# A four-direction selective scan on one core: transposes in place of products, and the 24 units of a chunk and their side jobs in another order

## The chip, the cores and the metric

The kernel runs on one core of a Trainium2 chip. The core has five engines that run their own instruction streams and meet only at semaphores: TensorE (PE; its weight loads are shown apart as PEld), VectorE (DVE), ScalarE (ACT), GpSimd (POOL) and SyncE (SP), which only issues DMAs here. SBUF is the working memory, PSUM takes TensorE's results. The metric is the device time of one execution in microseconds (us), and of several executions the median.

## The reference, cut to what matters

Layer 0 normalises x, projects it, convolves it, and then runs a selective scan over the 4096 pixels of each of 8 images, in four directions k (rows, columns, and both backwards). For each of 192 channels d and 16 states n:

```
delta = softplus(dt_proj(x_dbl) + bias)          # per channel and pixel
A     = -exp(A_logs)
h     = exp(delta * A) * h + (delta * u) * B     # over the pixels, one state per (d, n)
y     = sum over n of h * C
out   = y + u * D                                # the four directions are added at the end
```

B and C (16 values per pixel each) and the six inputs of `dt_proj` come from a projection of u with its own weights in each direction. A gated projection back to 96 channels and a second layer follow; the change touches neither.

## The kernel before

The program has three phases, one after the other: before the scan, the scan (`scan_phase`) and after it. Only the scan phase is changed. Its work is cut into 128 **chunks** (8 images, 4 directions, 4 pieces of TC = 1024 pixels). A chunk is two **steps** n, the even and the odd one, of 96 channels each. A step is 12 **units** x = 0 to 11, so a chunk has 24, which the prediction counts 0 to 23 (unit 12 is unit 0 of the odd step). A unit is a tile of 128 partitions by 1024 pixels: 32 channels (j = x mod 3) by 4 states (g, from the table `ORDER`).

What a unit costs on the engines depends on its kind (`KIND`):

- **Direct** (14 of 24): TensorE spreads B over the partitions into one of two PSUM tiles P (`fill`, 2 matmuls, L597), VectorE multiplies it with dt*u (`multiply`, L717), ScalarE makes the decay E (`exp`, L823), and VectorE runs the recurrence (`scan`, L739).
- **Diagonal** (6): TensorE makes the product itself, with 32 small matmuls of transposed dt*u (dluT) by diagonal copies of B (diag) (L639); VectorE only scans. These wait for `lt_copied` and `diag_made`.
- **Pooled** (4): GpSimd multiplies dt*u by B (L905) into one of two tiles dbu, ScalarE puts the decay into P; VectorE only scans, TensorE fills nothing.

After the scan GpSimd multiplies each H by C (`weigh`, L913), ScalarE saves the last column (`carry`, L829), and TensorE sums three units at a time into y (`sum_y`, L661; two halves in two iterations, in the third none; at the start of a step with one more matmul, L652 or L655).

The buffers that tie the engines together: P has 2 tiles, so the fill of unit un waits for the scan of un - 2 (`scan_done`); E has 3, H has 4 (a scan waits for `weigh` of un - 4), HC has 7, dbu has 2.

Once or twice a chunk come the **side jobs**. They go through one PSUM tile, `stage`, so each waits for ScalarE's copy of the one before (`held`): `project` (L581: B, C and dt inputs of the next chunk, a read of u that is strided for the odd directions), `delta` (L591, then softplus on ScalarE with a table load before and after, L773), `turn_b` (L610), `rep` 0 to 4 (L597: B or C spread over all partitions; the list `REPS` says which) and `turn_dlu` (L620: dt*u transposed, once a step). After `project` ScalarE copies twice (L763, L764) and VectorE takes the rounding rest (`split`, L711). ScalarE makes 32 diagonal copies a chunk (`diagonal`, L807), and GpSimd makes dt*u (`delta` in `pool`, L896), which goes out to DRAM and comes back spread over partitions (SP's queue).

Every engine's order is written out by hand: a loop over the units in which `if x == ...` says where each side job stands. TensorE's iteration un is: fill of unit un + 1, a half of `sum_y`, side jobs. Nothing overtakes anything on its engine.

Of the kernel before, what the change touches and what calls it, by code (L numbers as in the profile page):

```python
# [16 lines left out]
C = 96  # L17
# [291 lines left out]
def scan_phase(nc, ctx, T, S):  # L309
# [9 lines left out]
    DIAG_EVEN, DIAG_ODD = {0: 3, 1: 4, 2: 4, 3: 4}, {6: 3, 7: 3, 8: 3, 9: 3, 10: 2, 11: 3}  # L319
# [151 lines left out]
    for n in range(NSTEP):  # L471
        c = n // 2 + 1
        if n % 2 == 0:
            order += [("rep", c - 1, i) for i in range(3, 5) if n] + [("lt", n + 1)]
            order += [("x", c)] if c < NCHUNK else []
        elif c < NCHUNK:
            order += [("dt", n + 1), ("bt", c), ("rep", c, 0), ("lt", n + 1), ("dt", n + 2), ("rep", c, 1), ("rep", c, 2)]
# [6 lines left out]
    def sync(e):  # L484
# [62 lines left out]
        for n in range(NSTEP):  # L547
            if n % 2 == 0:
                if n:
                    in_dlr(n + 1)  # L550
                    out_dlu(n + 1)
                if ends_image(n + 1) and n + 2 < NSTEP:
                    load_u(n // 32 + 1)
                if n:
                    in_dur(n + 1)
                    store_y(n - 1)
                load_y(n + 1)
            else:
                if n + 1 < NSTEP:
                    out_dl(n + 1)  # L560
                    in_dlr(n + 1)
                store_y(n - 1)
                if n + 1 < NSTEP:
                    out_dlu(n + 1)
                    in_dur(n + 1)
# [6 lines left out]
    def tensor(e):  # L572
# [41 lines left out]
        def turn_dlu(m, sub):  # L614
# [63 lines left out]
        for un in range(NUNIT + 12):  # L678
# [7 lines left out]
            if n % 2 == 0:  # L686
                if x < 2 and n:
                    rep(c - 1, x + 3)
# [5 lines left out]
            elif c < NCHUNK:  # L694
                if x == 1:
                    delta(n + 1)
                if x == 5:
                    turn_b(c)
                if x == 6:
                    rep(c, 0)  # L700
                if x in (7, 8):
                    turn_dlu(n + 1, x - 7)
                if x == 9:
                    delta(n + 2)
                if x in (10, 11):
                    rep(c, x - 9)

    def vector(e):
# [40 lines left out]
        for un in range(NUNIT):  # L749
# [5 lines left out]
            if c < NCHUNK and n % 2 == 0 and x == 11:  # L755
# [967 lines left out]
```

## Time and profile before

| | |
|---|---|
| median of 3 runs | 12439.41 us (12432.49 to 12442.36) |
| the profiled execution | 12428.21 us, its span 12426.3 us |
| busy | DVE 86%, PE 86%, POOL 78%, ACT 65% |
| the scan phase in the span | from 662 to 10517 us |
| mean granted TensorE clock | 0.851 of full |

A matmul in fp32 stands in the profile as two instructions. A row of the timeline is: start, length, engine, line, operation, names (out<-in), shapes, count, and in brackets the idle time of the engine before it and what ended that. Waits are put down to what came last. PE spans are modelled at their ends, so a PE busy of 86% does not mean a full engine.

### The profile page before, as it was taken

To read this page: it belongs to the slowest core of one execution; us is meant where nothing else is said; L and a number is where in the kernel's file an instruction comes from. 1 tells how busy PE (TensorE), PEld (TensorE's weight loads), DVE (VectorE), ACT (ScalarE), POOL (GpSimd) and SP (SyncE) were. 2 spreads that over 40 slices of the span, in tenths; PEclk is the share of its full clock that TensorE was granted. 3 is DMA by queue.
4 is the path that set the end of the run, shared out by engine and by line. 5 is a ranking of instruction groups with operands and counts; after the bars stand their busy time and mean duration, and the time that the engine had idled before them with its cause. 6 is when DMAs were issued, how large, how long until landed. Compare 5 with 4: busy or idle time off the path is not lost. (4 is left out here: it accounts for less than half of the span.)

```text
span 12426.3 us, 236253 instructions
## 1 busy us (share of the span) xinstructions
PE 10745.4 (86%) x91896; PEld 5926.8 (48%) x91896; DVE 10724.7 (86%) x6806; ACT 8061.8 (65%) x13314; POOL 9752.4 (78%) x4238
## 2 busy tenths in 40 slices
PE   8978888888888888888888888888888887799999
PEld 5644444444444444444444444444444443678778
DVE  7789999999999999999999999999999998555554
ACT  3366777677777776777677767776777775444443
POOL 2178999899999999999999989998999998433330
PEclk9977888788878887888788878887888887799999
DMA  3344554455445554555455545544554454221220
GB/s 107 110 111 113 123 133 114 111 123 133 115 112 129 133 116 112 128 132 116 112 129 132 118 109 128 132 113 114 124 130 113 115 123 116 68 62 47 62 62 11
DMA packets 380191, 1363.70 MB, mean 110 GB/s; under 512 B 55270, under 2 KB 55974, under 8 KB 375756
## 3 DMA queue, kind: packets, MB, share of 16 engines
q1 hardware_dynamic: 379084, 1348.57, 46.0%
q8 instruction: 739, 12.11, 0.4%
q14 instruction: 368, 3.01, 0.1%
HBM read 983.45 MB, written 364.90 MB: 109 GB/s over the span
## 5 line engine op out<-in xcount | busy, mean ns | idle before, releaser
L913 POOL TENSOR_TENSOR HC<-H,crep 128x1024 f32<-128x1024 f32 x3072 | 7213.5, 2371 | 836.0 <-DVE H L739 831.4
L739 DVE TENSOR_TENSOR_SCAN H<-E,car,psum 128x1024 f32<-128x1024 f32 x1920 | 4479.2, 2343 | 232.0 <-PE psum L639 174.1
L823 ACT ACTIVATE E<-dlr,am 128x1024 f32<-128x1024 f32 x2560 | 2917.0, 1142 | 68.0 <-DVE H L739 65.6
L597 PE MATMUL psum<-sx,selb 96*128 96x512 f32 x4864 | 2192.0, 560 | 694.9 <-DVE H L739 419.9
L661 PE MATMUL psum<-HC,sely 128*32 128x512 f32 x12288 | 2519.3, 706 | 5.9 <-POOL HC L913 5.1
L639 PE MATMUL psum<-diag,dluT 128*32 128x128 f32 x49152 | 1933.2, 317 | 681.4 <-DVE H L739 676.0
L717 DVE TENSOR_TENSOR psum<-dur,psum 128x1024 f32<-128x1024 f32 x1792 | 2167.9, 1210 | 179.4 <-PE psum L597 175.2
L639 PEld LDWEIGHTS psum<-diag,dluT 128*32 128x32 f32 x49152 | 1624.4, 128 | 1307.2 <-DVE H L739 1176.5
L597 PEld LDWEIGHTS psum<-sx,selb 96*128 96x128 f32 x4864 | 1016.5, 242 | 2141.1 <-DVE H L739 862.5
L739 DVE TENSOR_TENSOR_SCAN H<-E,psum 128x1024 f32<-128x1024 f32 x640 | 1455.1, 2283 | 89.6 <-PE psum L639 68.7
L807 ACT ACTIVATE diag<-idn,blt 128x128 f32<-128x128 f32 x4096 | 1335.4, 394 | 4.1
L823 ACT ACTIVATE psum<-dlr,am 128x1024 f32<-128x1024 f32 x512 | 572.6, 1118 | 1117.9 <-DVE H L739 1116.4
L905 POOL TENSOR_TENSOR dbu<-dur,brep 128x1024 f32<-128x1024 f32 x512 | 1212.6, 2368 | 0.0
L739 DVE TENSOR_TENSOR_SCAN H<-psum,car,dbu 128x1024 f32<-128x1024 f32 x384 | 892.5, 2324 | 0.0
L661 PEld LDWEIGHTS psum<-HC,sely 128*32 128x32 f32 x12288 | 404.3, 119 | 1000.9 <-issue 936.8
L896 POOL TENSOR_TENSOR dlu<-dlt,u 96x1024 f32<-96x1024 f32 x256 | 673.2, 2630 | 133.3 <-ACT dlt L773 133.3
L581 PE MATMUL psum<-u,wx 96*102 96x512 f32 x1024 | 712.6, 824 | 29.1 <-DMA u<-scr_xa 29.1
L829 ACT COPY car<-H 128x1 f32<-128x1 f32 x2304 | 417.5, 181 | 482.8 <-DVE H L739 475.0
L620 PEld LDWEIGHTS psum<-idn,dlu 96*128 96x128 f32 x4096 | 530.9, 206 | 372.3 <-issue 249.0
L620 PE MATMUL psum<-idn,dlu 96*128 96x96 f32 x4096 | 596.6, 298 | 70.9 <-ACT brep L780 70.2
L591 PE MATMUL psum<-dlt,dtw 6*96 6x512 f32 x1024 | 597.4, 709 | 4.3 <-DVE sx L711 3.4
L1568 POOL TENSOR_TENSOR y<-y,tmp 96x1024 f32<-96x1024 f32 x64 | 195.1, 3114 | 458.0 <-DMA tmp<-scr_yk 458.0
(135 smaller groups left out, 11216.4 us busy)
## 6 DMA issues: line engine op xcount, KB each, us to landing
dur<-scr_dlu SPq DMA_DIRECT2D x1024, 384.0 KB, 6.8
dlr<-scr_dl SPq DMA_DIRECT2D x1024, 384.0 KB, 6.8
scr_dl<-dlt SPq DMA_DIRECT2D x256, 384.0 KB, 3.0
scr_dlu<-dlu SPq DMA_DIRECT2D x256, 384.0 KB, 6.8
scr_yk<-yt SPq DMA_DIRECT2D x256, 384.0 KB, 8.3
yp<-scr_yk SPq DMA_DIRECT2D x128, 384.0 KB, 8.8
scr_xa<-xs SPq DMA_DIRECT2D x64, 384.0 KB, 3.5
scr_sz<-xs SPq DMA_DIRECT2D x64, 384.0 KB, 3.4
```

Of the source, the lines that this page charges most:

```text
L581: r = e.matmul(stage[0:C + NR, sub * 512:(sub + 1) * 512], wx[:, k, h, :], view(k, h, t0, 512), start=h == 0, stop=h == 1)
L597: r = e.matmul(o[:, sub * 512:(sub + 1) * 512], selb[:, which, :], sx[:, c % 2, sub * 512:(sub + 1) * 512], start=True, stop=True)
L620: r = e.matmul(stage[:, sub * 512 + k * C:sub * 512 + (k + 1) * C], dlu[:, t0:t0 + 128], idn[0:C, 0:C], start=True, stop=True)
L639: r = e.matmul(P[un % 2][32 * q:32 * q + 32, i * 128:(i + 1) * 128], dluT[:, m % 2, i, 32 * j:32 * j + 32], diag[:, i, q, :], start=True, ...
L661: r = e.matmul(yps[32 * j:32 * j + 32, cols], sely[:], HC[:, (3 * i + j) % NHC, cols], start=g == 0 and k == 1, stop=g == NG - 1)
L717: e.tensor_tensor(P[un % 2], dur[:, slot(m, j), :], P[un % 2], ALU.mult).then_inc(mul_done)
L739: e.tensor_tensor_scan(H[:, un % NH, ::step], decay[:, ::step], drive[:, ::step], init, ALU.mult, ALU.add).then_inc(scan_done)
L807: e.mul(diag[:, i // 4, i % 4, :], idn[:], blt[:, i:i + 1]).then_inc(diag_made)
L823: e.activation(o, dlr[:, slot(m, j), :], ACT.Exp, scale=am[:, ae:ae + 1]).then_inc(exp_done)
L896: e.tensor_tensor(shaped(dlu[:], k), shaped(dl, k), view(k, half, t_of(k, ci), TC), ALU.mult).then_inc(dlu_made)
L905: e.tensor_tensor(dbu[:, p % NDB, :], dur[:, slot(m, j), :], brep[:], ALU.mult).then_inc(pool_mul_done)
L913: e.tensor_tensor(HC[:, un % NHC, :], H[:, un % NH, :], crep[:, g, :], ALU.mult).then_inc(hc_done)
```

## The change

Four things, all in `scan_phase`:

1. `turn_dlu` on TensorE issues `transpose` in place of `matmul` by the identity, as many and with the same operands.
2. `ORDER` and `KIND`: the units come in another order. There are still 14 direct, 6 diagonal and 4 pooled ones. Diagonal were units 5, 7, 9, 13, 15, 17 and are 5, 6, 10, 13, 15, 17. Pooled were 8, 10, 14, 16 and are 3, 8, 12, 16. `REPS` changes the order in which C's four groups are spread (1, 0, 3, 2 before, 2, 1, 0, 3 now).
3. The side jobs stand at other units, on TensorE, ScalarE and GpSimd. Both halves of `project` stand behind the fill of unit 11; before, one stood in front of it. `split` on VectorE stands behind scan 12 in place of scan 11. GpSimd makes the products for units 12 and 16 one after the other.
4. The 32 diagonal copies of ScalarE were dealt out in threes and fours from x = 6 of the odd step to x = 3 of the even; now they are 3, 16, 3, 3 (odd x = 4, 6, 8, 10) and 3, 4 (even x = 2, 3), and 25 in place of 17 before the first unit.

```diff
-    ORDER = ((1, 0, 0, 0, 2, 3, 2, 3, 1, 3, 1, 2), (1, 3, 1, 3, 1, 3, 0, 0, 0, 2, 2, 2))
+    ORDER = ((2, 0, 0, 1, 1, 3, 3, 2, 1, 0, 3, 2), (1, 3, 0, 3, 1, 3, 2, 2, 2, 0, 0, 1))
...
-                 for row, pooled in zip(ORDER, ((8, 10), (2, 4))))
-    REPS = (None, 1, 0, 3, 2)
+                 for row, pooled in zip(ORDER, ((3, 8), (0, 4))))
+    REPS = (None, 2, 1, 0, 3)
...
-                r = e.matmul(stage[:, sub * 512 + k * C:sub * 512 + (k + 1) * C], dlu[:, t0:t0 + 128], idn[0:C, 0:C],
-                             start=True, stop=True)
+                r = e.transpose(stage[:, sub * 512 + k * C:sub * 512 + (k + 1) * C], dlu[:, t0:t0 + 128], idn[0:C, 0:C])
...
@@ tensor, even step @@
+                if x == 2 and n > 1:
+                    rep(c - 1, 3)
+                if x == 4 and n > 1:
+                    rep(c - 1, 4)
+                if x == 6:
+                    turn_dlu(2 * (c - 1) + 1, 0)
                 if x == 7:
-                    turn_dlu(n + 1, 0)
-                    turn_dlu(n + 1, 1)
-                if x in (9, 10) and c < NCHUNK:
-                    project(c, x - 9)
+                    turn_dlu(2 * (c - 1) + 1, 1)
+                if x == 10 and c < NCHUNK:
+                    project(c, 0)
+                    project(c, 1)
@@ tensor, odd step @@
+                if x == 1 and c < NCHUNK:
+                    delta(2 * c)
+                if x == 2 and c < NCHUNK:
+                    turn_b(c)
+                if x == 3 and c < NCHUNK:
+                    rep(c, 0)
+                if x == 7 and c < NCHUNK:
+                    turn_dlu(2 * c, 0)
+                    turn_dlu(2 * c, 1)
+                if x == 8 and c < NCHUNK:
+                    delta(2 * c + 1)
+                if x == 10 and c < NCHUNK:
+                    rep(c, 1)
+                    rep(c, 2)
@@ vector @@
-            if c < NCHUNK and n % 2 == 0 and x == 11:
+            if c < NCHUNK and n % 2 == 1 and x == 0:
                 split(c)
@@ scalar, odd step @@
+                if x == 1 and c < NCHUNK:
+                    delta(2 * c)
...
+                if x == 10 and c < NCHUNK:
+                    delta(2 * c + 1)
+                    rep(c, 1)
+                    diagonal(c, 22, 3)
@@ pool, even step @@
+                if x == 0:
+                    multiply(24 * (c - 1) + 3)
+                if x == 2:
+                    multiply(24 * (c - 1) + 8)
+                if x == 7:
+                    multiply(24 * (c - 1) + 12)
+                    multiply(24 * (c - 1) + 16)
@@ pool, odd step @@
+                if x == 1 and c < NCHUNK:
+                    delta(2 * c)
+                if x == 10 and c < NCHUNK:
+                    delta(2 * c + 1)
```

Three places of the instruction streams, in the second chunk. Names: L639 and L650 are the matmuls of a diagonal unit, L597 and L609 those of a direct fill (or of a `rep`), L661 and L672 a half of `sum_y`, L652 and L663 its extra matmul, L620 and L632 `turn_dlu`, L581 and L593 `project`, L591 and L603 `delta`.

TensorE from the fill of unit 4 to that of unit 7, before:

```order
L597 MATMUL psum<-sx,selb 128x512 x2
L661 MATMUL psum<-HC,sely 32x512 x3
L639 MATMUL psum<-diag,dluT 32x128 x32
L597 MATMUL psum<-sx,selb 128x512 x2
L652 MATMUL psum<-u,dg 96x512
L661 MATMUL psum<-HC,sely 32x512 x3
L639 MATMUL psum<-diag,dluT 32x128 x32
```

The same place now (the first row is `rep` 3 and the fill of unit 4 in one, and the third after it `rep` 4):

```order
L609 MATMUL psum<-sx,selb 128x512 x4
L672 MATMUL psum<-HC,sely 32x512 x3
L650 MATMUL psum<-diag,dluT 32x128 x32
L609 MATMUL psum<-sx,selb 128x512 x2
L650 MATMUL psum<-diag,dluT 32x128 x32
L663 MATMUL psum<-u,dg 96x512
L672 MATMUL psum<-HC,sely 32x512 x3
L609 MATMUL psum<-sx,selb 128x512 x2
```

The diagonal fills of units 5 and 6 now follow each other with `rep` 4 between them, where a direct fill stood between two diagonal ones.

TensorE from `turn_dlu` of the even step to `delta` in the odd one, before:

```order
L620 MATMUL psum<-idn,dlu 128x96 x8
L639 MATMUL psum<-diag,dluT 32x128 x32
L661 MATMUL psum<-HC,sely 32x512 x6
L581 MATMUL psum<-u,wx 102x512 x2
L597 MATMUL psum<-sx,selb 128x512 x2
L581 MATMUL psum<-u,wx 102x512 x2
L597 MATMUL psum<-sx,selb 128x512 x2
L661 MATMUL psum<-HC,sely 32x512 x3
L639 MATMUL psum<-diag,dluT 32x128 x32
L661 MATMUL psum<-HC,sely 32x512 x3
L591 MATMUL psum<-dlt,dtw 96x512 x2
```

The same place now:

```order
L632 MATMUL psum<-idn,dlu 128x96 x8
L609 MATMUL psum<-sx,selb 128x512 x2
L672 MATMUL psum<-HC,sely 32x512 x3
L650 MATMUL psum<-diag,dluT 32x128 x32
L672 MATMUL psum<-HC,sely 32x512 x3
L609 MATMUL psum<-sx,selb 128x512 x2
L593 MATMUL psum<-u,wx 102x512 x4
L672 MATMUL psum<-HC,sely 32x512 x3
L650 MATMUL psum<-diag,dluT 32x128 x32
L672 MATMUL psum<-HC,sely 32x512 x3
L609 MATMUL psum<-sx,selb 128x512 x2
L603 MATMUL psum<-dlt,dtw 96x512 x2
```

The fill of unit 11 (the L609 row in front of L593) is no longer behind a half of `project`, and the whole `project` stands behind it.

VectorE from `split` to the fourth unit of the odd step, before (the order prints a scan as SCALAR_TENSOR_TENSOR; a scan from dbu is a pooled unit's):

```order
L711 TENSOR_TENSOR sx<-psum,sx 32x1024
L717 TENSOR_TENSOR psum<-dur,psum 128x1024
L739 SCALAR_TENSOR_TENSOR H<-E,car,psum 128x1024 x2
L739 SCALAR_TENSOR_TENSOR H<-psum,car,dbu 128x1024
L739 SCALAR_TENSOR_TENSOR H<-E,car,psum 128x1024
```

The same place now:

```order
L756 SCALAR_TENSOR_TENSOR H<-psum,car,dbu 128x1024
L728 TENSOR_TENSOR sx<-psum,sx 32x1024
L756 SCALAR_TENSOR_TENSOR H<-E,car,psum 128x1024
L734 TENSOR_TENSOR psum<-dur,psum 128x1024
L756 SCALAR_TENSOR_TENSOR H<-E,car,psum 128x1024 x2
L756 SCALAR_TENSOR_TENSOR H<-psum,car,dbu 128x1024
```

The split comes one scan later, and unit 15 (the second scan of the x2 row) now stands behind a direct unit, not behind a pooled one.

## Rows read from the trace of the kernel before

**Rows 1.** The page: busy time of the engines, share, instructions.

```profile
PE 10745.4 (86%) x91896; PEld 5926.8 (48%) x91896; DVE 10724.7 (86%) x6806; ACT 8061.8 (65%) x13314; POOL 9752.4 (78%) x4238
```

**Rows 2.** The scan phase in the windows view: PE, PEld, DVE, ACT, POOL busy, clock.

```profile
662.00:10517.00 9855.00, 8409.95 (x74177) 4112.29 (x74176) 9258.61 (x4991) 7000.67 (x11762) 9027.65 (x3838) 0.83 0.52 120
```

**Rows 3.** The waits view: who waited for whom, us, times, longest.

```profile
DVE H L739 <- PE psum L639: 242.9, 260, 1.6
...
DVE psum L717 <- PE psum L597: 175.2, 121, 28.4
DVE sx L711 <- ACT sx L764: 141.7, 66, 20.5
```

**Rows 4.** The page's groups: GpSimd's weighing.

```profile
L913 POOL TENSOR_TENSOR HC<-H,crep 128x1024 f32<-128x1024 f32 x3072 | 7213.5, 2371 | 836.0 <-DVE H L739 831.4
```

**Rows 5.** Timeline of VectorE, units 11 to 18 of an odd direction.

```profile
5394.80 1.23 DVE L717 TENSOR_TENSOR psum<-dur,psum 128x1024 f32<-128x1024 f32 x1 [1.14 <-PE psum L597]
...
5400.29 1.22 DVE L711 TENSOR_TENSOR sx<-psum,sx 32x1024 fp32r<-32x1024 f32 x1 [1.87 <-ACT sx L764]
...
5411.15 2.35 DVE L739 TENSOR_TENSOR_SCAN H<-E,car,psum 128x1024 f32<-128x1024 f32 x1 [1.52 <-PE psum L639]
5413.42 2.32 DVE L739 TENSOR_TENSOR_SCAN H<-psum,car,dbu 128x1024 f32<-128x1024 f32 x1
5415.66 2.32 DVE L739 TENSOR_TENSOR_SCAN H<-E,car,psum 128x1024 f32<-128x1024 f32 x1
5417.90 1.21 DVE L717 TENSOR_TENSOR psum<-dur,psum 128x1024 f32<-128x1024 f32 x1
5419.14 2.35 DVE L739 TENSOR_TENSOR_SCAN H<-E,car,psum 128x1024 f32<-128x1024 f32 x1
```

**Rows 6.** Timeline of TensorE in the same chunk and the next.

```profile
5407.44 3.64 PE L639 MATMUL psum<-diag,dluT 128*32 128x128 f32 x64 [3.31 <-DVE H L739]
...
5413.55 1.95 PE L639 MATMUL psum<-diag,dluT 128*32 128x128 f32 x64 [0.34 <-DVE H L739]
...
5453.74 3.64 PE L639 MATMUL psum<-diag,dluT 128*32 128x128 f32 x64 [1.87 <-DVE H L739]
...
5464.66 2.02 PE L620 MATMUL psum<-idn,dlu 96*128 96x96 f32 x16
...
5470.21 3.66 PE L581 MATMUL psum<-u,wx 96*102 96x512 f32 x4
...
5474.17 3.60 PE L581 MATMUL psum<-u,wx 96*102 96x512 f32 x4
```

**Rows 7.** Windows around those fills; the column behind POOL's is the granted clock.

```profile
5407.40:5411.80 4.40, 4.36 (x70) 3.35 (x73) 2.88 (x2) 4.34 (x6) 4.40 (x3) 0.50 0.23 61
5411.80:5425.00 13.20, 11.61 (x116) 5.97 (x110) 13.13 (x8) 10.12 (x20) 13.20 (x7) 1.00 0.78 191
...
5453.70:5459.60 5.90, 5.86 (x68) 4.27 (x68) 5.54 (x3) 4.21 (x6) 5.90 (x3) 0.50 1.03 211
```

**Rows 8.** Timeline of ScalarE: table load, four diagonal copies, cast behind project, next exp.

```profile
5410.06 1.28 ACT L823 ACT_TABLE_LOAD   x1
...
5446.80 1.28 ACT L807 ACTIVATE diag<-idn,blt 128x128 f32<-128x128 f32 x4
...
5478.82 1.01 ACT L764 CAST sx<-psum 96x1024 fp32r<-96x1024 f32 x1
5479.73 1.15 ACT L823 ACTIVATE E<-dlr,am 128x1024 f32<-128x1024 f32 x1
```

**Rows 9.** Timeline of TensorE, units 22 and 23 of an odd direction.

```profile
6121.40 2.02 PE L620 MATMUL psum<-idn,dlu 96*128 96x96 f32 x8
6123.13 1.20 PE L597 MATMUL psum<-sx,selb 96*128 96x512 f32 x2
6124.26 1.93 PE L661 MATMUL psum<-HC,sely 128*32 128x512 f32 x6
6126.12 3.73 PE L591 MATMUL psum<-dlt,dtw 6*96 6x512 f32 x4
```

More of the change, by code:

```diff
@@ L473, in scan_phase @@
         if n % 2 == 0:
-            order += [("rep", c - 1, i) for i in range(3, 5) if n] + [("lt", n + 1)]
+            order += [("rep", c - 1, 3)] if n > 1 else []
+            order += [("rep", c - 1, 4)] if n > 1 else []
+            order += [("lt", 2 * (c - 1) + 1)]
             order += [("x", c)] if c < NCHUNK else []
-        elif c < NCHUNK:
-            order += [("dt", n + 1), ("bt", c), ("rep", c, 0), ("lt", n + 1), ("dt", n + 2), ("rep", c, 1), ("rep", c, 2)]
+        else:
+            order += [("dt", 2 * c)] if c < NCHUNK else []
+            order += [("bt", c)] if c < NCHUNK else []
+            order += [("rep", c, 0)] if c < NCHUNK else []
+            order += [("lt", 2 * c)] if c < NCHUNK else []
+            order += [("dt", 2 * c + 1)] if c < NCHUNK else []
+            order += [("rep", c, 1)] if c < NCHUNK else []
+            order += [("rep", c, 2)] if c < NCHUNK else []
     for job, last in zip(order[1:], order):
@@ L550, in sync @@
                     in_dlr(n + 1)
+                if n:
                     out_dlu(n + 1)
@@ L851, in scalar @@
         exp(0)
-        diagonal(0, 0, sum(DIAG_ODD.values()))
+        diagonal(0, 0, 25)
         for un in range(NUNIT + 12):
@@ L863, in scalar @@
             if n % 2 == 0:
-                if x < 3 and n:
-                    rep(c - 1, x + 2)
-                if x in DIAG_EVEN:
-                    diagonal(c - 1, sum(DIAG_ODD.values()) + sum(DIAG_EVEN[i] for i in range(x)), DIAG_EVEN[x])
-                if x == 8:
-                    turn_dlu(n + 1)
+                if x == 0 and n > 1:
+                    rep(c - 1, 2)
+                if x == 1 and n > 1:
+                    rep(c - 1, 3)
+                if x == 2:
+                    diagonal(c - 1, 25, 3)
+                if x == 3:
+                    diagonal(c - 1, 28, 4)
+                if x == 6 and n > 1:
+                    rep(c - 1, 4)
+                if x == 9:
+                    turn_dlu(2 * (c - 1) + 1)
                 if x == 11 and c < NCHUNK:
                     project(c)
-            elif c < NCHUNK:
-                if x == 2:
-                    delta(n + 1)
-                if x == 6:
+            else:
+                if x == 1 and c < NCHUNK:
+                    delta(2 * c)
+                if x == 3 and c < NCHUNK:
                     turn_b(c)
-                if x == 7:
+                if x == 4 and c < NCHUNK:
                     rep(c, 0)
-                if x == 8:
-                    turn_dlu(n + 1)
-                if x == 10:
-                    delta(n + 2)
-                if x == 11:
+                    diagonal(c, 0, 3)
+                if x == 6 and c < NCHUNK:
+                    diagonal(c, 3, 16)
+                if x == 7 and c < NCHUNK:
+                    turn_dlu(2 * c)
+                if x == 8 and c < NCHUNK:
+                    diagonal(c, 19, 3)
+                if x == 10 and c < NCHUNK:
+                    delta(2 * c + 1)
                     rep(c, 1)
-                if x in DIAG_ODD:
-                    diagonal(c, sum(DIAG_ODD[i] for i in range(6, x)), DIAG_ODD[x])
+                    diagonal(c, 22, 3)
     def pool(e):
```

32 lines of the change are left out of this document (7 added, 25 removed).

## The prediction, made before the changed kernel had run

> **What bounds the kernel now.** I read the page's busy line first. TensorE and VectorE stand at 86% each [rows 1], which names no bound, so I took the scan phase alone [rows 2]: in 9855.0 us VectorE works 9258.6, GpSimd 9027.7, TensorE 8410.0, ScalarE 7000.7. VectorE is the bound, and the most that any order of the same work can win is what it stands idle there: 9855.0 - 9258.6 = 596 us, 4.7 us in each of the 128 chunks. GpSimd would be next, only 231 us behind. What lies outside the phase is untouched.
>
> Then the waits view, for who makes VectorE idle [rows 3]: the diagonal fills of TensorE 243 us, its direct fills 175 (28 of it one wait at the start), ScalarE's cast in front of split 142 (20.5 of it one wait). It never waits for GpSimd. The timeline says where in a chunk [rows 5]. Unit 15, diagonal, waits 1.52 us at 5411.15; I counted 127 such waits, one in nearly every chunk, of some 1.4 us: 177 of the 243. Units 5 and 9 wait shorter, in some 150 cases. The product of unit 11 waits 1.14 us and split 1.87, but nearly only where the next chunk's direction is odd, 64 times: 3.1 us each, 198 together. A second wait for a direct fill, at unit 23, comes 36 times with some 1.8 us, 64 together.
>
> Two things decide whether a diagonal unit waits. One is the window: its fill may start when the scan two units before ends, so TensorE has as long as the unit between them takes on VectorE. From the starts in rows 5, that is 2.26 us for a diagonal or a pooled unit (5413.42 to 5415.66) and 1.24 + 2.26 = 3.50 for a direct one. The other is the clock. The same 64 instructions take 1.95 us at 5413.55 and 3.64 at 5407.44 and 5453.74 [rows 6], and the granted clock is 1.00 and 0.50 there [rows 7], TensorE's 2.4 and 1.2 GHz. With some 0.2 us for the hand-over, a fill fits into 2.26 us at the upper level and misses by 1.6 at the lower; behind a direct unit it misses by 0.35 at most. What TensorE did before the clock was low: it stood idle 3.31 us and 1.87 us in front of those two fills. It got the upper level back 4.4 and 5.9 us after it had begun again [rows 7].
>
> **The change part by part**, in us a chunk, counted on VectorE from start to start.
>
> *Unit 15.* It now stands behind a direct unit. 1.4 goes. What is late next is its exp: ScalarE's `delta` of the odd step stands at unit 13 in place of 14, and the exp of unit 15 is queued behind softplus and the table load. From the end of scan 12: in even directions TensorE is through fill 14 and delta by +3.5; softplus and exp at 1.15 each with the table load of 1.28 between them [rows 8] give +7.1, and VectorE is there at +7.0. In odd directions all of this hangs on the project before it and comes 0.5 late. 0.1 x 64 + 0.5 x 64 = 38 us.
>
> *Project and split.* The fill of unit 11 is no longer behind a half of project, so that wait goes. Both halves now start when fill 11 is out, 0.9 us after scan 9. A half in an odd direction takes 3.60 us to its end, and the next can start after about 2.7 (the 3.66 us of the one at 5470.21 overlap what follows) [rows 6]: 0.9 + 2.7 + 3.6 = 7.2, and ScalarE's two copies of 1.01 each [rows 8] give 9.3. VectorE is ready for split after units 10 (diagonal), 11 (direct) and 12 (pooled): 2.26 + 3.50 + 2.24 = 8.0. So 1.3 is left of 3.1: 1.3 x 64 = 83 us. In even directions there was hardly a wait here before, and split has a scan more of room now.
>
> *Units 5 to 7.* Here the new order is worse. Unit 3 is pooled and needs no fill, so TensorE, done with the fill of unit 2, a half of sum_y and rep 3 some 3.4 us after scan 0, has nothing until scan 2 has ended, 7.0 us after scan 0: about 3.6 us idle, as long as the gap that stood in front of the slow fill at 5407.44. From the end of scan 2 (0.0), at the lower level: fill 4 to 1.3 (1.20 [rows 9]), a half of sum_y to 3.3 (1.93 [rows 9]), then fill 5. The upper level comes back 4.4 to 5.9 after the restart, so at about 5.1; half of fill 5 runs slowly, and it ends at 6.1, where VectorE wanted it at 2.24 + 3.50 = 5.7: 0.5 lost with the hand-over. Rep 4 (0.65, half of a low row) and fill 6 (1.95) end at 8.7 for 8.5: 0.3. The larger half of sum_y (2.0) and fill 7 end at 11.4 for 11.1: 0.4. Together 1.2 x 128 = 154 us. Bounds: nothing, if the clock stays up; 6.3 a chunk (1.3, 2.5, 2.5 by the same steps at the lower level throughout), 806 us.
>
> *The other diagonal units.* 13 and 17 have the short window, 10 a long one. Before, 13 and 17 had it too and lost next to nothing. I take 0.2, 26 us.
>
> *Units 21 to 23.* What made unit 23 late is a sequence at the lower level: half a turn 2.02, fill 1.20, sum_y 1.93, delta 3.73 [rows 9]. Now delta stands one unit earlier, behind a whole turn. At the upper level it fits. At the lower one, fill 20 and 21, the turn, sum_y and delta take up to 1.1 us too much. I take it for less than half of the chunks: 50 us, bounds 0 and 141.
>
> *Transposes.* 16 instruction pairs of a turn take 2.02 us at the upper level [rows 6]. The trace shows no transpose. Bounds: as long as now, 0; or, at most, 2.0 us less twice a chunk. Neither end moves VectorE by itself, since the turns have cover: ScalarE's copy is awaited by nobody for several units. I take half of the time and no gain, but for units 21 to 23, where it is in the 50. The Trainium skill (TensorE: Matmul & The Clock Gate, Part 4: PE-mode transpose) says that a transpose does not count as busy for the clock as a matmul does. No row here shows one; it is a rival below.
>
> *GpSimd.* Same work, 2.37 us a tile [rows 4]. Two multiplies in a row (for units 12 and 16) put it back: from the start of the chunk it ends weigh 7 at about 31.5 us, and scan 11 (H has 4 buffers) wants that at 33.5. Slack 2.0, all else is wider: 0.
>
> *ScalarE's diagonals.* Four take 1.28 us [rows 8], so 16 in a row about 5, behind which exp 20 still has some 0.8 us: 0. Before the first unit 8 more stand on the path: 2.4 us, once.
>
> **Sum.** Idle left: 38 + 83 + 154 + 26 + 50 = 351 us where 596 stood: -245, +2 at the start. From the profiled execution's own 12428.2: 12185. The median of the runs shown is 11.2 above that execution, so the forecast in its terms is **12196 us**, 2.0% less.
>
> **The rivals.**
>
> *The clock does not fall at the start of a chunk, or comes back sooner.* Then units 5 to 7 cost 0 to 40 us: 12196 - 115 to 154, about 12060. For it: before, units 5 and 9 lose on average only 0.4 a chunk, with gaps of up to 1.9 us around. Against: the gap is twice that.
>
> *Transposes count as idle.* If turning leaves the clock low behind it, delta and fills 22 and 23 run at 1.2 GHz in every chunk, 1.1 instead of 0.4, and unit 10 loses the 0.35 of a long window: 0.7 + 0.35, some 135 us: 12330. The Trainium skill's page named above would have it so. For it from rows: the turn stands between two waits with fill 20 alone beside it. Against: its neighbours sum_y, delta and project are dense.
>
> *GpSimd or ScalarE becomes the bound.* GpSimd has 231 us less to do than VectorE and more waiting in its order: crep for group 0 is spread third but used by unit 1, and weigh 1 then waits about 0.5 us. If its lag outgrows the 2.0 us at weigh 7, or exp 20 comes late, 1 us a chunk: 12196 + 128 = 12324.
>
> *Slower: the pair of diagonal units 5 and 6 runs at the lower level.* One mechanism: no fill for unit 3, idle TensorE, low clock, and two diagonal fills with one short window. If the upper level is not back before fill 6, the price is 3 to 6.3 a chunk. It turns the sign where the pair costs more than 1.2 + 243 / 128 = 3.1, that is if the clock comes back some 9 us after the restart in place of 4.4 to 5.9; a price of 4.5 gives 12196 + 3.3 x 128 = 12618. For it: the fills are followed by waits, which are what lowered the clock before. Against: rows 7.
>
> *The change doesn't do what it says:* if transposes are issued as the same two passes, nothing moves by them; that is in the forecast.
>
> **How the numbers follow.** Forecast 0.46; clock stays up 0.20; transposes idle 0.13; GpSimd or ScalarE 0.09; slower 0.12. The likeliest's own range is 12120 to 12290. The whole range, with at most 0.2 left out, takes in the first three rivals and ends in front of the fourth: 12040 to 12440. What a measurement of this kernel can tell from no change is 0.2%, 25 us, so faster means under 12414. The first four cases are all below it, but their tails reach it: faster 0.83, within 0.05, slower 0.12.
>
> **What would show it.** Right: unit 15 waits no more; VectorE's wait in front of the product of unit 11 is gone and the one for the cast stands at about 1.3 us, only in odd directions; new waits for diagonal fills at units 5 and 6, with a granted clock of 0.50 behind a TensorE gap of about 3.6 us; VectorE's idle time in the scan phase about 350 us. Wrong: waits of VectorE for GpSimd's weighing, an exp that comes late, direct fills late by more than 1 us at unit 22, or a clock of 0.50 behind every turn.

## The result, and the profile after

The changed kernel is slower by 0.3%: 12480.7 us (median of 9 runs) against 12446.23 us for the kernel before on the same chips, ratio 1.0028 with a 95% interval of 1.0016 to 1.0040. The forecast was 12196 us with a range to 12440. Its profiled execution has a span of 12464.6 us, 38.3 above that of before.

The busy line of its page, against [rows 1]:

```profile
PE 10542.2 (85%) x89848; PEld 5478.0 (44%) x89848; DVE 10742.0 (86%) x6806; ACT 8078.1 (65%) x13314; POOL 9756.1 (78%) x4238
```

Its scan phase in the windows view, against [rows 2]:

```profile
662.00:10555.00 9893.00, 8208.53 (x72134) 3666.26 (x72134) 9270.20 (x4991) 7016.16 (x11761) 9029.51 (x3837) 0.82 0.52 120
```

VectorE has the same instructions, is busy 12 us longer with them, and stands idle 9893.0 - 9270.2 = 623 us where 596 were forecast to become 351. TensorE has 2048 instructions fewer: in the profile a transpose is one, an fp32 matmul two. The waits view of VectorE, against [rows 3]:

```profile
DVE H L756 <- PE psum L650: 183.2, 254, 2.2
DVE psum L734 <- PE psum L609: 149.1, 195, 26.2
DVE sx L728 <- ACT sx L781: 147.0, 65, 20.6
DVE H L756 <- ACT car L846: 64.6, 77, 1.3
DVE H L756 <- ACT E L840: 32.0, 25, 4.9
DVE H L756 <- POOL HC L939: 17.0, 7, 4.4
```

Diagonal fills cost 60 us less than before, but ScalarE, to which 10 us of the waits for H were put down before, now costs 97 (the two rows with "ACT"). By unit, counted from the starts on VectorE's timeline (a gap of over 0.03 us beyond the usual one), in us over the 128 chunks:

| wait in front of | before | after | forecast for after |
|---|---|---|---|
| unit 15 | 180 | 90 | 38 |
| product of unit 11; scan 11 | 79; 0 | 0; 16 | 0; 0 |
| split | 129 | 132 | 83 |
| units 5, 6, 7 | 28, 0, 0 | 45, 38, 39 | 154 together |
| unit 9 | 55 | 0 | 0 |
| units 10, 13, 17 | 0, 1, 1 | 0, 38, 72 | 26 together |
| units 22, 23 | 0, 66 | 91, 0 | 50 together |
| in all, small ones too | 551 | 575 | 351 |

The waits at the product of unit 11 and at units 9 and 23 are gone. That at unit 15 is halved and not gone, and split waits as long as before. The new waits stand where the forecast put them, except the 16 us at scan 11. It is mostly the sizes that were wrong.

VectorE in one odd chunk of the changed kernel, against [rows 5]:

```profile
5413.98 2.32 DVE L756 TENSOR_TENSOR_SCAN H<-psum,car,dbu 128x1024 f32<-128x1024 f32 x1
5418.06 1.22 DVE L728 TENSOR_TENSOR sx<-psum,sx 32x1024 fp32r<-32x1024 f32 x1 [1.76 <-ACT sx L781]
5420.66 2.35 DVE L756 TENSOR_TENSOR_SCAN H<-E,car,psum 128x1024 f32<-128x1024 f32 x1 [1.38 <-PE psum L650]
...
5427.68 2.35 DVE L756 TENSOR_TENSOR_SCAN H<-E,car,psum 128x1024 f32<-128x1024 f32 x1 [1.17 <-ACT car L846]
...
5433.71 2.35 DVE L756 TENSOR_TENSOR_SCAN H<-E,car,psum 128x1024 f32<-128x1024 f32 x1 [1.44 <-PE psum L650]
...
5450.62 1.23 DVE L734 TENSOR_TENSOR psum<-dur,psum 128x1024 f32<-128x1024 f32 x1 [0.54 <-PE psum L609]
```

The same chunk on TensorE's timeline and, in the second fence, on ScalarE's. The first three of the five waits in brackets above are one chain:

```profile
5408.37 0.73 PE L609 MATMUL psum<-sx,selb 96*128 96x512 f32 x2 [0.70 <-DVE H L756]
5408.94 7.03 PE L593 MATMUL psum<-u,wx 96*102 96x512 f32 x8
...
5417.61 2.97 PE L650 MATMUL psum<-diag,dluT 128*32 128x128 f32 x62
...
5422.03 1.95 PE L603 MATMUL psum<-dlt,dtw 6*96 6x512 f32 x4
...
5430.08 3.55 PE L650 MATMUL psum<-diag,dluT 128*32 128x128 f32 x64 [0.41 <-DVE H L756]
```

```profile
5417.02 1.01 ACT L781 CAST sx<-psum 96x1024 fp32r<-96x1024 f32 x1
...
5424.02 1.11 ACT L790 ACTIVATE dlt<-psum,dtb 96x1024 f32<-96x1024 f32 x1 [2.43 <-PE psum L603]
5425.15 1.28 ACT L840 ACT_TABLE_LOAD   x1
5426.44 1.15 ACT L840 ACTIVATE E<-dlr,am 128x1024 f32<-128x1024 f32 x1
```

Project takes 7.03 us, so the cast ends at 5418.0 and split waits. The fill of unit 13 comes behind it and is slow (2.97 for 62 of its 64 instructions), so unit 13 waits. Delta follows that, softplus waits 2.43 us for it, and the exp of unit 15 is behind softplus and the table load. The fourth wait is unit 17's: its fill began as soon as scan 15 had ended (5430.08), but took 3.55 us. The releaser "ACT car" at 5427.68 is only the last semaphore ScalarE sent; the exp ends at 5427.6. The windows view of the stretch in which project and the fill of unit 13 ran shows the granted clock (the number behind POOL) at about 0.6 on average, which is a part at 1.00 and a part at 0.50:

```profile
5412.00:5417.50 5.50, 5.50 (x13) 1.13 (x14) 4.30 (x2) 1.48 (x2) 5.50 (x4) 0.58 0.00 1
5417.50:5420.50 3.00, 3.00 (x68) 2.70 (x65) 1.22 (x1) 2.98 (x6) 3.00 (x2) 0.62 0.00 0
```

This is no accident of one chunk, and the clock is not what makes project long. In all 64 chunks in front of one with an odd direction, where project's read of u is strided, the two halves in a row take 7.02 to 7.03 us, whether the granted clock over them averages 0.63 or 0.98 (in front of an even direction, 3.60). But in all 64 the clock falls from 1.00 to 0.50 before they end, though TensorE shows no idle time there. In the kernel before, where a fill stands between the halves, it fell in 2 of 64.

### The profile page after: what moved, and what is told of

Read it like the earlier page. It is cut to its first block and busy times, and to the rows that moved or that the text cites. A ratio compares the mean times of both kernels' runs of the same rounds, so it can differ in the third digit from the quotient of the medians.

```text
span 12464.6 us, 232157 instructions
## 1 busy us (share of the span) xinstructions
PE 10542.2 (85%) x89848; PEld 5478.0 (44%) x89848; DVE 10742.0 (86%) x6806; ACT 8078.1 (65%) x13314; POOL 9756.1 (78%) x4238
## 5 line engine op out<-in xcount | busy, mean ns | idle before, releaser
L609 PE MATMUL psum<-sx,selb 96*128 96x512 f32 x4864 | 2074.0, 523 | 1495.4 <-DVE H L756 1330.8
L672 PE MATMUL psum<-HC,sely 128*32 128x512 f32 x12288 | 2640.9, 726 | 34.2 <-POOL HC L939 34.2
L609 PEld LDWEIGHTS psum<-sx,selb 96*128 96x128 f32 x4864 | 913.9, 229 | 3306.6 <-DVE H L756 2045.8
L650 PE MATMUL psum<-diag,dluT 128*32 128x128 f32 x49152 | 1902.7, 309 | 157.4 <-DVE H L756 142.8
L650 PEld LDWEIGHTS psum<-diag,dluT 128*32 128x32 f32 x49152 | 1587.7, 125 | 830.1 <-DVE H L756 587.9
L824 ACT ACTIVATE diag<-idn,blt 128x128 f32<-128x128 f32 x4096 | 1278.8, 389 | 70.1 <-PE psum L650 66.1
L803 ACT COPY crep<-psum 128x1024 f32<-128x1024 f32 x512 | 517.3, 1010 | 573.0 <-PE psum L609 513.9
L672 PEld LDWEIGHTS psum<-HC,sely 128*32 128x32 f32 x12288 | 373.6, 118 | 980.9 <-issue 814.1
L603 PE MATMUL psum<-dlt,dtw 6*96 6x512 f32 x1024 | 725.9, 844 | 5.4 <-DVE sx L728 3.4
L593 PE MATMUL psum<-u,wx 96*102 96x512 f32 x1024 | 682.9, 816 | 28.9 <-DMA u<-scr_xa 28.9
L1321 PEld LDWEIGHTS psum<-w2s,hs 128*100 128x100 f32 x4800 | 447.3, 168 | 15.2
```

The costliest lines, as they stand in the source:

```text
L593: r = e.matmul(stage[0:C + NR, sub * 512:(sub + 1) * 512], wx[:, k, h, :], view(k, h, t0, 512), start=h == 0, stop=h == 1)
L603: r = e.matmul(stage[0:C, sub * 512:(sub + 1) * 512], dtw[C:C + NR, k * ND + half * C:k * ND + (half + 1) * C], dts[:, sub * 512:(sub + 1) ...
L609: r = e.matmul(o[:, sub * 512:(sub + 1) * 512], selb[:, which, :], sx[:, c % 2, sub * 512:(sub + 1) * 512], start=True, stop=True)
L650: r = e.matmul(P[un % 2][32 * q:32 * q + 32, i * 128:(i + 1) * 128], dluT[:, m % 2, i, 32 * j:32 * j + 32], diag[:, i, q, :], start=True, ...
L672: r = e.matmul(yps[32 * j:32 * j + 32, cols], sely[:], HC[:, (3 * i + j) % NHC, cols], start=g == 0 and k == 1, stop=g == NG - 1)
L824: e.mul(diag[:, i // 4, i % 4, :], idn[:], blt[:, i:i + 1]).then_inc(diag_made)
```

## The experiments

All times are medians, and all ratios are to the kernel before in runs on the same chip.

| kernel | us | ratio (95% interval) |
|---|---|---|
| before_transposes | 12336.45 | 0.9906 (0.9894 to 0.9919) |
| after_products | 12441.16 | 0.9997 (0.9988 to 1.0006) |
| after_turn_twice | 12442.77 | 0.9980 (0.9971 to 0.9990) |
| after_delta_later | 12435.44 | 0.9987 (0.9978 to 0.9995) |
| after_project_before | 12325.52 | 0.9899 (0.9884 to 0.9913) |
| after_project_delta | 12422.31 | 0.9972 (0.9962 to 0.9983) |
| after_b_later | 12501.37 | 1.0033 (1.0020 to 1.0045) |
| after_gap_filled | 12508.28 | 1.0040 (1.0028 to 1.0053) |
| before_project_late | 12296.43 | 0.9873 (0.9857 to 0.9888) |
| before_pooled_12 | 12249.96 | 0.9832 (0.9818 to 0.9845) |
| pooled_12_earlier | 12170.30 | 0.9771 (0.9758 to 0.9784) |
| pooled_12_products | 12304.30 | 0.9883 (0.9866 to 0.9899) |

**The two halves of the change apart.** The kernel before with only the transposes, and the changed kernel with only its order.

```diff
 # before_transposes
-                r = e.matmul(stage[...], dlu[:, t0:t0 + 128], idn[0:C, 0:C], start=True, stop=True)
+                r = e.transpose(stage[...], dlu[:, t0:t0 + 128], idn[0:C, 0:C])
 # after_products: the same edit backwards, on the changed kernel
```

> The kernel before with the 16 turns of two steps as TensorE transposes, nothing moved. Theory A (less work on TensorE makes its clock fall): a turn gets shorter, from 2.02 to 0.82 us, but TensorE then waits longer for the scan, the granted clock falls more often, and the fills behind are late: 0 to 60 us slower than before, 12440 to 12500. Rival B (the shorter turn helps): the waits of units 9 and 23, in front of which a turn stands, go, 60 to 120 us faster, 12330 to 12385, and the slowness of the changed kernel comes from its order alone.

> The changed kernel with its turns as products again: the new order alone. Theory A: TensorE has 1.2 us more to do behind the fill of unit 20, does not stand idle for 2.1 us there, and delta behind it runs in about 1.95 us, not 3.73; the wait at unit 22 (95 us) goes, and those of unit 13 and split (project at the low clock) get smaller: 100 to 200 us faster than the changed kernel, 12280 to 12380, so faster than before. Rival B: the turn is only longer, nothing else changes: 12480 to 12560.

The transposes alone make the kernel before 0.94% faster (theory B). The order alone makes no difference that can be measured. Together they are slower than either. A whole turn, 8 transposes, takes 0.82 us, where 8 products, 16 instructions, took 2.02 in [rows 6]. The changed kernel on TensorE's timeline, in the chunk in an odd direction that is shown above and in one in an even direction:

```profile
5440.17 0.82 PE L632 MATMUL psum<-idn,dlu 96*128 96x96 f32 x8
5443.12 0.80 PE L609 MATMUL psum<-sx,selb 96*128 96x512 f32 x2 [2.12 <-DVE H L756]
5443.85 1.93 PE L672 MATMUL psum<-HC,sely 128*32 128x512 f32 x6
5445.71 3.73 PE L603 MATMUL psum<-dlt,dtw 6*96 6x512 f32 x4
...
5052.36 0.82 PE L632 MATMUL psum<-idn,dlu 96*128 96x96 f32 x8
5055.23 1.22 PE L609 MATMUL psum<-sx,selb 96*128 96x512 f32 x2 [2.05 <-DVE H L756]
5056.38 1.93 PE L672 MATMUL psum<-HC,sely 128*32 128x512 f32 x6
5058.24 3.72 PE L603 MATMUL psum<-dlt,dtw 6*96 6x512 f32 x4
```

TensorE stands idle 2.12 and 2.05 us behind the short turn, and sum_y and delta behind it run at the lower level; the fill of unit 22 is late behind them. The same chunk in the even direction in after_products, on TensorE's timeline. The idle time is shorter and delta faster:

```profile
5045.70 1.92 PE L632 MATMUL psum<-idn,dlu 96*128 96x96 f32 x16
5048.57 0.74 PE L609 MATMUL psum<-sx,selb 96*128 96x512 f32 x2 [0.95 <-DVE H L757]
5049.23 1.06 PE L673 MATMUL psum<-HC,sely 128*32 128x512 f32 x6
5050.22 3.16 PE L603 MATMUL psum<-dlt,dtw 6*96 6x512 f32 x4
```

Delta takes over 3 us in all 126 chunks counted of the changed kernel and in 75 of them here. Unit 22 waits 55 us here and 91 with transposes; in even directions 8 and 44, in odd ones 48 with both. In the kernel before the turns stand in front of units 9 and 23, and there transposes take 43 and 15 us off the waits (55 to 12, 66 to 51). So theory A's clock effect is real, and smaller than expected (39 us between the medians, not 100 to 200), and theory B holds where something late is queued behind the turn. The 36 us at unit 22 are not the whole account: in the profiled execution of after_products, the slowest of its 12 (12477 us, with 25 us more than the changed kernel outside the scan phase), VectorE's idle time in the scan is only 17 us less than in the changed kernel, since units 5 and 6 and the product of unit 0 wait longer. In the kernel before, the transposes took 77 us off VectorE's idle time, 58 of them at units 9 and 23 and some 12 at unit 5.

**Do transposes count for the clock?** The changed kernel with the odd step's turn issued twice.

```diff
+                    turn_dlu(2 * c, 0)
                     turn_dlu(2 * c, 0)
+                    turn_dlu(2 * c, 1, False)
                     turn_dlu(2 * c, 1)
 # turn_dlu(m, sub, last=True): False leaves out the semaphore behind the first of the two
-            if sub:
+            if sub and last:
                 r.then_inc(lt_done)
```

> The changed kernel with the transposes of the odd step's turn issued twice: 1.6 us of TensorE's time in place of 0.8, near the 2.0 of the products, and the same result. Theory A (only the lack of work lowers the clock): like the products it keeps the clock up behind it and takes most of the 44 us away that unit 22 waits in even directions: 12420 to 12460. Rival I (transposes do not count as work for the clock): unit 22 waits as before or longer, 12475 to 12520.

The same chunk in the even direction on its TensorE timeline:

```profile
5040.94 1.48 PE L632 MATMUL psum<-idn,dlu 96*128 96x96 f32 x16
5043.82 0.73 PE L609 MATMUL psum<-sx,selb 96*128 96x512 f32 x2 [1.40 <-DVE H L758]
5044.48 1.06 PE L672 MATMUL psum<-HC,sely 128*32 128x512 f32 x6
5045.47 2.09 PE L603 MATMUL psum<-dlt,dtw 6*96 6x512 f32 x4
```

Doing needless transposes made the kernel 0.5% faster than the changed one (ratios 0.9980 and 1.0028, from different chips but each against the kernel before). Delta takes 2.09 us in this chunk, near its 1.95 at the upper level; but over 3 us, as in the changed kernel, in 83 of 126 chunks, among them the one in the odd direction. Unit 22's wait in even directions falls from 44 to 9, as with products. Units 5 and 6 wait some 35 us longer in this profiled execution, and why is not known. So extra transposes kept the clock up in about a third of the chunks, which they could not have done if they were as good as idle time for it; what lowered it was that there was less to do. The Trainium skill (TensorE: Matmul & The Clock Gate, Part 4: PE-mode transpose) says that a transpose does not count as busy in the way that a matmul does. These runs fit that only if a transpose still has some weight; how much beside a matmul, no run here shows.

**Unit 15.** ScalarE's delta behind exp 15.

```diff
 # scalar, odd step
-                if x == 1 and c < NCHUNK:
+                if x == 2 and c < NCHUNK:
                     delta(2 * c)
```

> The changed kernel with ScalarE's delta of the odd step at unit 14, as before, in place of 13: the exp of unit 15 comes in front of softplus. Theory C (the exp queued behind softplus and the table load makes unit 15 wait): those 93 us go, dl and the job turn_b come 0.3 us later; what may come back is unit 17 in odd directions: 40 to 95 us faster than the changed kernel, 12385 to 12440. Rival D: the wait only moves to unit 17 through turn_b and rep 0, which wait for softplus: no change, 12460 to 12500.

The wait at unit 15 goes from 90 to 6 us, and unit 16, whose exp is now the one behind the table load, gets 40. Theory C, less what comes back; 0.4% faster than the changed kernel. The exp was not all of unit 15's wait: in even directions, where 13 of the 90 us lie, its fill ran at a mean granted clock below 0.9 in 51 of 63 chunks.

**Where project stands.** The first half in front of fill 11, as before; split stays behind scan 12.

```diff
 # tensor, even step
-                if x == 10 and c < NCHUNK:
-                    project(c, 0)
-                    project(c, 1)
+                if x in (9, 10) and c < NCHUNK:
+                    project(c, x - 9)
```

> The changed kernel with the first half of project in front of the fill of unit 11 again, the second behind it. In odd directions the cast comes 2.7 to 3.5 us earlier, so split's wait (135 us) goes, but the fill of unit 11, whose window is 2.26 us now (a diagonal unit before it), comes late by about 2 us. If both hold: about even, 12450 to 12510. If the late project matters mostly through split and unit 13: 50 to 100 us faster, 12380 to 12430.

1.3% faster than the changed kernel and 1.0% faster than the one before. Split 132 to 7, unit 13 38 to 10, unit 15 90 to 35, unit 5 45 to 12, unit 17 72 to 56; on the other side the product of unit 11, 0 to 113. The five that fall add up to 257 us, for 113 on the other side, and this one edit accounts for the sign. Split, 13 and 15 are the chain shown above. Unit 17 belongs to it by the clock: its waits from a slow fill (21 us in front of odd directions) fall to 5, those from a late one stay. How unit 5, most of a chunk later, gains from it was not followed. With the second half behind fill 11 alone, the clock falls during project in 1 of 64 chunks in place of all, and in none during the fill of unit 13, where it was low in 60.

> The changed kernel with both of the repairs that were tried apart: the first half of project in front of fill 11 (1.3% faster than the changed kernel) and ScalarE's delta behind exp 15 (0.4%). If the two are apart, 12280 to 12300. If the earlier project had already taken most of the wait of unit 15 (it fell from 90 to 35 us there), the rest is 35 less what unit 16 loses: 12310 to 12340.

Both repairs together are worse than project alone (12422 us): units 17 and 22 wait 102 us each (56 and 82 without) and unit 16 38. The two are not independent. Why units 5 and 22 lose with the later delta was not settled.

**Unit 17.** Turn_b and rep 0 behind its fill.

```diff
 # tensor, odd step
-                if x == 2 and c < NCHUNK:
+                if x == 4 and c < NCHUNK:
                     turn_b(c)
-                if x == 3 and c < NCHUNK:
+                if x == 5 and c < NCHUNK:
                     rep(c, 0)
 # scalar, odd step: turn_b at x == 5, rep(c, 0) and diagonal(c, 0, 19) at x == 6
```

> The changed kernel with turn_b and rep 0 behind the fill of unit 17 (TensorE at units 16 and 17 of the chunk in place of 14 and 15, ScalarE's copies and the first 19 diagonals with them). Theory G: unit 17 waits because TensorE has fill 15, two halves of sum_y, turn_b and rep 0 to do before it: its 72 us go in even directions at least, and the change is 40 to 90 us faster, 12390 to 12440. Rival H: unit 17 waits for the low clock, whatever stands before it; then nothing changes or TensorE's added idle time makes it worse: 12460 to 12540.

Theory G holds at its place: 72 to 27 us (even directions 51 to 12). The 72 have two parts, counted on both timelines: in 51 chunks the fill begins late, behind turn_b, rep 0 and sum_y (49 us), and in 15, as in the one shown above, it begins in time and is slow, at a granted clock of 0.53 (22 us). But the 19 diagonals now stand in one row on ScalarE, and the exp of unit 20 behind them is late by 126 us, so the kernel is slower. The waits view of VectorE in this kernel puts that down to "issue":

```profile
DVE H L756 <- PE psum L650: 158.0, 240, 2.7
DVE sx L728 <- ACT sx L781: 146.9, 65, 20.9
DVE H L756 <- issue: 121.8, 95, 1.8
```

Unit 22's wait is gone here (91 to 4).

**The gap at the start of a chunk.** Needless matmuls in it.

```diff
 # fill, direct
+                for _ in range(2 if un % 24 == 2 and un > 24 else 0):
+                    spread(P[un % 2], m // 2, 2 * g)
 # rep
+            for _ in range(1 if i == 3 and c else 0):
+                spread(stage, c, 2 * REPS[i] + 1)
```

> The changed kernel with work that nobody needs in TensorE's idle time at the start of a chunk: the fill of unit 2 three times and rep 3 twice, some 2.0 of the 3.7 us in front of the fill of unit 4, results unchanged. Theory L (the prediction's: the gap lowers the clock and the diagonal pair 5 and 6 is late by that): the granted clock stays up there and the waits of units 5 to 7, 122 us, fall to under 60: 12400 to 12440. Rival M (TensorE simply has too much to do between fill 5 and fill 7, at either clock): they stay over 90, 12460 to 12510.

This one did not settle its question. The gap in front of fill 4 only shrank, from a median of 4.5 us to 3.1, since TensorE must still wait for scan 2, and the clock fell behind it all the same. Here is the place in the changed kernel (fill 4, half of sum_y, fill 5, rep 4 and fill 6):

```profile
5468.31 1.22 PE L609 MATMUL psum<-sx,selb 96*128 96x512 f32 x2 [4.62 <-DVE H L756]
5469.45 1.93 PE L672 MATMUL psum<-HC,sely 128*32 128x512 f32 x6
5470.57 4.08 PE L650 MATMUL psum<-diag,dluT 128*32 128x128 f32 x64
...
5475.25 1.99 PE L650 MATMUL psum<-diag,dluT 128*32 128x128 f32 x64
```

And the kernel with the needless matmuls. Its TensorE timeline (fill 4, half of sum_y, fill 5):

```profile
5098.74 0.72 PE L609 MATMUL psum<-sx,selb 96*128 96x512 f32 x2 [3.23 <-DVE H L760]
5099.40 1.42 PE L676 MATMUL psum<-HC,sely 128*32 128x512 f32 x6
5101.01 3.08 PE L654 MATMUL psum<-diag,dluT 128*32 128x128 f32 x64 [0.20 <-DVE H L760]
```

Units 5 to 7 wait 149 us for 122, and the pooled unit 3, which waits in no other kernel of this order, waits some 40 for ScalarE's exp (24 times). So whether a clock that stays up would take the waits away stays open as an experiment. The changed kernel's trace says where to look. Fill 5 begins as soon as its tile is free and runs at a mean granted clock below 0.9 in all 127 chunks counted: unit 5 waits by the clock. Fill 6 runs at 1.00 in all of them and only begins late behind it. Unit 7 is another case: it waits 0.4 us in 96 chunks, and nearly the same in every kernel of this order, with the clock at 1.00 in front of it in 97% of them. They are the chunks of the three directions in which sum_y, between fill 6 and fill 7, has its extra matmul of 1 us; in the fourth direction unit 7 does not wait.

**The same moves in the order of before.** First project and split late.

```diff
 # before_project_late, from before_transposes
-                if x in (9, 10) and c < NCHUNK:
-                    project(c, x - 9)
+                if x == 10 and c < NCHUNK:
+                    project(c, 0)
+                    project(c, 1)
...
-            if c < NCHUNK and n % 2 == 0 and x == 11:
+            if c < NCHUNK and n % 2 == 1 and x == 0:
                 split(c)
```

> The kernel before with transposes (12336 us in its own run) and one more part of the change: both halves of project behind the fill of unit 11 and split behind scan 12. Unit 12 is direct in this order, so split comes 9.2 us after scan 9 and the cast about 9.3. Theory E (moving project back only pays where the units behind it give it cover; in the changed order the pooled unit 12 takes 1.26 us of it away): the waits at unit 11 and split, 207 us together, fall to under 70 and unit 15 stays as it is: 12170 to 12260. Rival F (project late makes the rest of the step late in any order, as units 13, 15 and 17 in the changed kernel): 12300 to 12400.

40 us faster than before_transposes, where 76 to 166 were expected. Split's wait goes (129 to 10) and so does unit 11's, but here unit 12 is direct, its fill stands behind the project, and it waits 186 us. The expectation had overlooked that fill. It also shows what the pooled unit 12 of the changed order is for: it has no fill to be late. So the next kernel takes it over, and with it a direct unit in front of 15:

```diff
 # before_pooled_12, from before_project_late
-                 for row, pooled in zip(ORDER, ((8, 10), (2, 4))))
+                 for row, pooled in zip(ORDER, ((8, 10), (0, 4))))
 # pool, even step
-                if x == 11:
-                    multiply(12 * (n + 1) + 2)
+                if x == 10:
+                    multiply(12 * (n + 1))
```

> The kernel of before_project_late with unit 12 pooled in place of unit 14, the place that the changed kernel gives it, and GpSimd's product for it one unit earlier; unit 15 then has a direct unit in front. If the window alone decides (the prediction's step): unit 15's 173 us go, split's wait in odd directions comes to about 1.3 us (83 us) again: 12100 to 12200. If project behind unit 11 makes exp 15 and fill 13 late as in the changed kernel, 100 to 150 of it come back: 12200 to 12300.

Unit 15 falls from 123 to 17 us. What is late now is GpSimd's product for unit 12. VectorE's timeline shows the wait in one chunk:

```profile
5016.36 2.35 DVE L739 TENSOR_TENSOR_SCAN H<-psum,car,dbu 128x1024 f32<-128x1024 f32 x1 [1.73 <-POOL dbu L905]
```

and its waits view the sum:

```profile
DVE H L739 <- POOL dbu L905: 170.5, 110, 2.2
```

One unit earlier it may stand without waiting for its tile:

```diff
-                if x == 10:
+                if x == 9:
                     multiply(12 * (n + 1))
```

> The kernel of before_pooled_12 (12250 us) with GpSimd's product for unit 12 one unit earlier still, behind weigh 8, where its tile dbu is just free. In before_pooled_12 the scan of unit 12 waited 188 us for that product. Theory J (only its place in GpSimd's order made it late): the 188 us go, split and unit 13 take back up to 60 since project now ends against them: 12080 to 12160. Rival K (GpSimd has no room at all there, as its busy time is 230 us below VectorE's): the wait moves to a weigh, 12200 to 12260.

All of that wait goes, 81 us come back at split, and the kernel is at 12170 us, 2.3% faster than before and the best of all. VectorE's waits view in it:

```profile
DVE sx L711 <- ACT sx L764: 137.1, 65, 20.9
DVE H L739 <- PE psum L638: 83.3, 136, 1.5
DVE psum L717 <- PE psum L597: 60.1, 41, 26.2
DVE H L739 <- issue: 37.1, 105, 0.4
```

Last, what the transposes are worth in it:

> The fastest version so far (pooled_12_earlier, 12170 us) with its turns as products again. It has the turns where the kernel before has them, one in front of the fill of diagonal unit 9 and one, in halves, in front of delta and unit 23. Theory N (what a transpose is worth depends on what is queued behind the turn; these places are the ones where it paid 114 us before): 60 to 130 us slower, 12230 to 12300. Rival O (the transposes' gain came from project's old place and is used up): within 30 us of 12170.

Products cost 134 us here, even a little over the 114 in the kernel before: unit 23 waits 141 us with products and 30 with transposes, unit 9 44 and 25. Theory N.

## Why the prediction was wrong

**Bound, windows, places: right.** VectorE's idle time was the measure, and the units named were those that waited. GpSimd took no part but for 7 waits at unit 11 (17 us, up to 4.4 each), all in the last chunk of an image, where its cover of 2.0 us was not enough.

**"0.9 + 2.7 + 3.6 = 7.2 ... So 1.3 is left of 3.1": the first link of the chain that turned the sign.** Project took 7.03 us where 2.7 + 3.6 = 6.3 were reckoned. The 2.7 was read from a half behind which a fill comes next; a second half begins 3.42 us after the first, in every one of the 64 chunks and at either clock. Project ended 7.8 us after scan 9 (which ended at 5408.2) and the second copy at 9.8, not 9.3. Split waits 1.8 in place of 1.3 in front of odd directions, and some in front of even ones: 132 us for 83. The prediction also had nothing on what two halves in a row do to the clock: it falls while they run, and the fill of unit 13 behind them is slow by that.

**"In odd directions all of this hangs on the project before it and comes 0.5 late": the size.** Fill 13, delta, softplus and exp 15 are one chain behind project. Fill 13 took 2.97 instead of 1.95 and the wait was 1.2, not 0.5; in even directions it was 0.2 on average, not 0.1, and from a slow fill, not from the exp: 90 us for 38. after_project_before took 55 of it away and 28 of unit 13's 38, which shows that they belong to project.

**"The other diagonal units ... I take 0.2": a term that was not worked out.** It rested on 13 and 17 having lost nothing before. But the new order puts turn_b, rep 0 and two halves of sum_y between fill 15 and fill 17, and project in front of fill 13. 110 us for 26. That is the largest single miss, 84 us. For unit 17 two thirds of it are the queue in front of the fill and one third the slow fill; for unit 13 it is project.

**Units 21 to 23: right mechanism, half the size.** 91 us for 50. The wait comes in 98 chunks, not in "less than half". The cause is in part the transposes themselves: "neither end moves VectorE by itself" was wrong. They took 1.1 us of work away, the clock was low behind the longer idle time in every chunk, and with products 36 us of the wait go (after_products; after_turn_twice agrees).

**Units 5 to 7: 122 us for 154**, the only large term that was sized well. The granted clock was 0.50 behind the gap, as forecast, and the gap longer: 2.8 to 4.6 us, in the median 4.5, for 3.6. Units 5 and 6, priced at 0.8 a chunk, wait 0.65. Unit 7 waits the forecast's 0.4, but only in the 96 chunks with the larger half of sum_y.

**Transposes, taken as no gain.** The row of 2.02 us in [rows 6] is 16 instructions, which are 8 products and not 16 pairs as the prediction has it; no term rests on that. In the order of before the transposes are a gain of 114 us. The turn at unit 7 stands there in front of the diagonal fill 9, and the second half turn in front of delta. The prediction looked at who awaits the turn's result and not at what is queued behind it on TensorE. In the new order TensorE waits for a scan behind most turns, so a shorter one only makes that wait longer.

**Of the rivals**, none came as told. The slower one had its mechanism in units 5 and 6, which wait only 0.65 us a chunk; the slowness came from a sum: 49 + 52 + 84 + 41 + 16 us over the five terms of split, 15, 10/13/17, 22 and 11, less 32 at 5 to 7, which is 210 of the 272 by which VectorE's idle time (623) passed the forecast's 351. Another 45 was a slip in the sum: of the 596 us idle before, only 551 are waits in the table, and the other 45, gaps too small to count, had no term though nothing was to remove them. They are still there (48). VectorE's busy time, 12 us up, had no term either, and why it rose is not known. "Transposes count as idle" foretold a low clock behind every turn. That came behind the odd step's turn, in 126 of 126 chunks, but behind the even step's in 33 of 127; and its reason does not hold, since after_turn_twice shows that more transposes raise the clock. "The clock does not fall" is refuted by the rows of the changed kernel.

## What to carry to other kernels

In a hand-written order, a side job that is moved costs along the whole chain behind it on its engine and on those it feeds, not only at the wait it is moved to; follow it to the third link, at the slower clock too. Take the price of two operations in a row from two that stand in a row: the first of two halves cost 2.7 us in front of a fill and 3.42 in front of its like. Where a product is made cheaper, ask what is queued behind it: there it pays, elsewhere it only makes idle time. A term of the form "lost nothing before" holds only if what stands in front of it is the same.

## What the runs showed of the hardware

The fp32 transpose of a 96x128 tile is one instruction in the profile and the product by the identity two (2048 for 4096), and 8 transposes take 0.82 us where 8 products take 1.92 to 2.02. Adding 8 needless transposes to a turn made the whole kernel faster: in a third of the chunks TensorE's granted clock stayed up over what follows, so that the next matmuls took 2.09 in place of 3.72 us.

An fp32 projection with a strided read of its moving operand takes 7.02 to 7.03 us for two halves in a row, against 3.60 with the contiguous read, and the same at both levels of the clock. While it ran, the granted clock fell to 0.50 in all 64 chunks of the changed kernel, in 62 of before_project_late and in 63 of pooled_12_earlier, with no idle time of TensorE in it; with a fill between the halves it fell in 2 of 64 (before) and 1 of 64 (after_project_before).
